# A selective-scan and mixture-of-experts block on one core: moving the z projection to the experts' idle PSUM banks, and the next sequence's norms and four GpSimd steps to other slots

## The chip, the core and the metric

The kernel runs on one core of a Trainium2 chip. The metric is the device time of one execution in microseconds (us). The core has TensorE (matmuls, results in the eight PSUM banks), VectorE, ScalarE and GpSimd for the element-wise work, and SyncE (SP), which issues the DMAs. Each engine runs its own list of instructions in order; between engines there are only semaphores.

## The reference

For each of 16 sequences of 512 rows and 128 columns:

```
h  = layernorm(x) * (1 + ca) + sa                    # sa, ca, ga, sb, cb, gb: one row each per sequence
xn = layernorm(h) * norm_g + norm_b
x  = x + ga * (h + mamba_f(xn) + flip(mamba_b(flip(xn))))
h  = layernorm(x) * (1 + cb) + sb
x  = x + gb * (sum over 8 experts, top 2 weighted, + one shared expert: (silu(h w1) * (h w2)) w3)

mamba(xn): u, z = split(xn Win);  u = silu(conv4(u));  dt_r, B, C = split(u Wx)
           dt = softplus(dt_r Wdt + b);  h_t = exp(dt_t A) h_(t-1) + dt_t u_t B_t   (256 channels x 16 states)
           y = (sum over states of h_t C_t + u D) * silu(z);  result y Wout
```

All data are 32-bit floats. silu(z) is computed as z/2 times (1 + tanh(z/2)); the factor one half is in the transposed weights wzT.

## The kernel before, in words

**Passes and slots.** The program runs 17 passes (`passes`, L303). Pass b does the scan of sequence b and, beside it, the experts of sequence b-1. A pass is a loop over 32 slots (STEPS), and each engine has its own copy of the loop (the functions `body`). A slot is one state n of one direction d: slots 0 to 15 are the forward direction, 16 to 31 the backward one. In the text "s29" is slot 29, and a slot runs from the start of its first scan on VectorE (L923) to the next slot's.

**What every slot has.** ScalarE writes exp(dt A) for the next slot into the two banks of psA (L675, one instruction for each half of the channels; each waits until VectorE has read that half). GpSimd multiplies v = dt u by a broadcast row of B into bt (L490), at most two slots ahead, because bt has two buffers. VectorE scans both halves in place (L923, twice), then multiplies each by a row of C into g (L933, twice). TensorE transposes g and adds it up in psY (L1181). SP loads the rows of B and C, two states with one DMA each (L389, L393).

**The experts.** In 18 of the slots TensorE computes an up projection into F0 and F1 (L1281, L1289; UP_SLOTS is 7 to 27 without 9, 10 and 22). One slot later ScalarE takes the tanh from F0 (L757) and copies F1 (L760), VectorE makes pf between its two read-outs (L1022), and GpSimd makes act (L580). The down projection goes to F2 (L1329). F0 and F1 hold nothing from s29 to s6.

**The preparation.** While a sequence is scanned, the next direction is prepared through one shared PSUM bank, psP, whose pieces are taken in a fixed order (pP_full, pP_free). PREP_SLOT is (19, 0): the forward direction of sequence b+1 is prepared from s19 of pass b, the backward one of sequence b from s0. Counted from there: u half 0 and half 1 at 0 to 5 (convolution as four matmuls, L1197; L693, L696; VectorE L963), the B, C and dt rows at 6 (L1205, L705), dt halves at 7 and 8 (L1210, L712 to L716), the logarithm at 9 (`ln1p`, L723, which loads a table of functions before it, and `preload_act_table` after it, L724), z halves at 9 and 11 (TensorE L1214 into psP, ScalarE tanh L696, VectorE zs one slot later, L963), dt at 10 on GpSimd (`make_dt`, L534), v at 11 (`make_v`, L539).

**The norms of sequence b+1** are also done in pass b: statistics on VectorE at s8 and s13 (L939, L943), their inverse roots on GpSimd at s9 and s14 (`moments`, L497 to L502), z1 and xn on ScalarE at s10 and s15 (L728), the modulation on GpSimd at s12 (L516, L518), the transposes and xnT at s16 (L1236, L745), hx on GpSimd at s21 (L522) and s23 (L525). The gated output weights wg are made on GpSimd at s25 (L595) from modG; SP's list has its DMA at s4, behind the loads of C rows that wait for the read-outs of s5 (L419, L393).

**Order inside a slot.** ScalarE: expert tanh and copy, exponentials of the next slot, ln1p, hxK, the experts' side work, then norms and preparation. GpSimd: bt of the next slot, then the output of sequence b-2 at s0, then `side` (wg, norms, dt, v), then `ffn_side` (act, xs). VectorE: two scans, first read-out, pf, second read-out, norms and preparation, the experts' side work, the gating of the forward direction. TensorE: sum of g of the slot before, the experts' side, down projection, post and preparation, up projection.

Of the kernel before, what the change touches and what calls it, by code (L numbers as in the profile page):

```python
# [21 lines left out]
U, XD, DT, Z = 0, 2, 3, 5  # L22
PREP = 7
# [55 lines left out]
def adaln_mamba_moe(nc, t, out):  # L79
# [3 lines left out]
    with ctx:  # L83
# [383 lines left out]
        def _(pool):  # L467
# [36 lines left out]
            def norms(b, slot):  # L504

                if slot == RSTD_SLOT:
                    if isinstance(b, int) and b == 0:
# [4 lines left out]
                if slot == H1_SLOT:
                    pool.wait_ge(zA, 8 * b + 4)
                    pool.wait_ge(modA_in, 16 * b + 16)
                    wait(pool, pP_full, xn_piece(b - 1) + 1)
                    g.tensor_tensor(xn[:, :, :], z1[:, :, :], over_tiles(modA[:, 1, :]), ALU.mult).then_inc(h1_s, 1)  # L516
                    pool.wait_ge(h1_s, 2 * b + 1)
                    g.tensor_tensor(z1[:, :, :], xn[:, :, :], over_tiles(modA[:, 0, :]), ALU.add).then_inc(h1_s, 1)  # L518
                if slot == HX_SLOT:

                    wait(pool, hxK_s, b)
                    g.tensor_tensor(hx[:, :, :], z1[:, :, :], over_tiles(modA[:, 2, :]), ALU.mult).then_inc(hx_s, 1)  # L522
                if slot == HX_SLOT + 2:
# [75 lines left out]
            def side(b, slot, prep_b, prep_f, post_f):  # L599
                if post_f and slot == WG_SLOT:  # L600
                    gated_weights(b)
                if prep_f is not None:
                    norms(prep_f, slot)
                    if slot == PREP_SLOT[0] + DT_AT + 3:
                        make_dt(prep_f, 0)
                    if slot == PREP_SLOT[0] + V_AT:
                        make_v(prep_f, 0)
                if prep_b and slot == PREP_SLOT[1] + DT_AT + 3:
                    make_dt(b, 1)
                if prep_b and slot == PREP_SLOT[1] + V_AT:  # L610
# [6 lines left out]
            norms(0, HX_SLOT)  # L617
            norms(0, HX_SLOT + 2)
# [25 lines left out]
        def _(act_e):  # L644
# [43 lines left out]
            def silu(b, d, kind, half):  # L688

                at = (0 if kind == U else 2) + half  # L690
                take(b, piece(d, kind, half))
                if kind == U:
                    s.activation(psP[:, :], psP[:, :], ACT.Identity, scale=0.5,  # L693
                                 bias=convb[d][:, half:half + 1]).then_inc(xh_s, 1)
                    act_e.wait_ge(xh_s, 4 * b + 2 * d + half + 1)
                s.activation(th[:, at, :], psP[:, :], ACT.Tanh).then_inc(th_s, 1)  # L696

            def prep(b, d, k):

                if k - U_AT in (1, 4):  # L700
                    silu(b, d, U, (k - U_AT) // 3)
# [15 lines left out]
                if k - Z_AT in (0, 2):  # L717
                    silu(b, d, Z, (k - Z_AT) // 2)
# [113 lines left out]
            first_z(F2[:, :], 0)  # L832
            first_z(psP[:, :], 1)
# [36 lines left out]
        def _(dve):  # L870
# [83 lines left out]
            def silu(b, d, kind, half):  # L954
                at = (0 if kind == U else 2) + half
                dve.wait_ge(th_s, 8 * b + 4 * d + at + 1)
# [5 lines left out]
                dst = (u if kind == U else zs)[d][:, half, :]  # L962
                w.scalar_tensor_tensor(dst, th[:, at, :], 1.0, psP[:, :], ALU.add, ALU.mult).then_inc(pP_free, 1)  # L963

            def prep(b, d, k):
                if k - U_AT in (2, 5):
                    silu(b, d, U, (k - U_AT - 2) // 3)
                if k - Z_AT in (1, 3):
                    silu(b, d, Z, (k - Z_AT) // 2)

            def gate_y(b, d, half):
# [8 lines left out]
                dve.wait_ge(pP_free, PIECES * b + piece(d, Z, 1) + 1)  # L980
# [164 lines left out]
        def _(pe):  # L1145
# [264 lines left out]
```

## Time and profile before

| what | value |
|---|---|
| device time, median of 3 runs | 2459.84 us (2459.71 to 2462.65) |
| the profiled execution's own time | 2461.73 us |
| its span, first to last instruction | 2459.9 us |
| VectorE busy | 2236.6 us, 91% |
| TensorE busy | 2066.5 us, 84% |
| GpSimd busy | 2023.6 us, 82% |
| ScalarE busy | 1511.4 us, 61% |
| DMA engines busy (mean) | some 37% |
| mean granted TensorE clock | 0.927 of 2.4 GHz |

How to read it: the shares are averages over stages with different limits. A line of the timeline gives the start, the duration, the engine and line of the kernel, the operation with result and operands, how many in a row are merged, and in brackets how long the engine had been idle before it and what ended the wait. Scans start 0.09 us before the instruction ahead of them has ended; so do most pairs on VectorE and ScalarE.

### The profile page before, as it was taken

The numbers are of one execution on the slowest core, as the hardware profiler recorded it, in microseconds if no ns is written. First come the engines' busy times: TensorE is split into PE (matmuls) and PEld (weight loads), VectorE is DVE, ScalarE is ACT, GpSimd is POOL, SyncE is SP. The second block draws the span as 40 slices with busy tenths as digits, with TensorE's granted clock in tenths as the row PEclk, the third lists the DMA queues.
The fourth block names the chain that finished last, engine by engine and source line by source line (L and its number), as shares of the span: only waits on it lengthen the run. The fifth ranks groups of instructions, "written<-read, shape, count | busy, mean of one in ns | idle before, by whom it ended". The sixth has DMA issues, their size and how long they took to land. (4 is left out here: it accounts for less than half of the span.)

```text
span 2459.9 us, 31865 instructions
## 1 busy us (share of the span) xinstructions
PE 2066.5 (84%) x9957; PEld 1312.1 (53%) x9957; DVE 2236.6 (91%) x3546; ACT 1511.4 (61%) x2483; POOL 2023.6 (82%) x1334
## 2 busy tenths in 40 slices
PE   6678988889888887978888898887978888898868
PEld 2445655545555554655555565554655555465545
DVE  4999999999999999999999999999999999999962
ACT  4656666576656666666676656666666576666633
POOL 2777979889798897979889797897979889797855
PEclk7678989989899999999999898999999999999989
DMA  5333343333444334333433334333433343333310
GB/s 149 131 136 122 134 135 132 136 122 126 135 133 135 122 126 134 135 134 129 140 123 125 134 130 143 126 121 126 140 134 127 133 129 125 129 135 136 123 67 27
DMA packets 124061, 312.42 MB, mean 127 GB/s; under 512 B 19700, under 2 KB 46308, under 8 KB 123892
## 3 DMA queue, kind: packets, MB, share of 16 engines
q1 hardware_dynamic: 123892, 310.39, 37.2%
q8 instruction: 79, 1.29, 0.2%
q14 instruction: 90, 0.74, 0.1%
HBM read 303.74 MB, written 6.60 MB: 126 GB/s over the span
## 5 line engine op out<-in xcount | busy, mean ns | idle before, releaser
L490 POOL TENSOR_TENSOR bt<-v,bb 128x1024 f32<-128x1024 f32 x511 | 1207.0, 2363 | 181.9 <-DVE psA L923 167.2
L923 DVE TENSOR_TENSOR_SCAN psA<-psA,bt 128x512 f32<-128x512 f32 x1024 | 1196.6, 1214 | 56.7 <-POOL bt L490 37.3
L675 ACT ACTIVATE psA<-dt,aneg 128x512 f32<-128x512 f32 x1024 | 689.3, 688 | 723.3 <-DVE g L933 723.1
L1181 PEld LDWEIGHTS psY<-ident,g 128*128 128x128 f32 x4096 | 509.4, 151 | 461.2 <-DVE g L933 256.0
L1181 PE MATMUL psY<-ident,g 128*128 128x128 f32 x4096 | 604.4, 292 | 166.4 <-DVE g L933 165.2
L933 DVE TENSOR_TENSOR g<-psA,cb 128x512 f32<-128x512 f32 x1024 | 672.6, 676 | 0.0
L580 POOL TENSOR_TENSOR act<-pf,gf 128x512 f32<-128x512 f32 x288 | 367.0, 1274 | 163.4 <-DVE pf L1022 151.0
L1281 PE MATMUL F<-h2T,w 128*128 128x512 f32 x576 | 325.5, 648 | 126.0 <-DVE pf L1022 125.9
L1329 PE MATMUL F<-w,act 128*128 128x128 f32 x2304 | 308.3, 277 | 13.6 <-POOL act L580 13.1
L1329 PEld LDWEIGHTS F<-w,act 128*128 128x128 f32 x2304 | 280.7, 192 | 31.1 <-POOL act L580 26.6
L1197 PE MATMUL psP<-xnT,wcT 128*128 128x512 f32 x496 | 258.2, 647 | 9.6 <-DVE zs L1085 9.2
L1022 DVE SCALAR_TENSOR_TENSOR pf<-tf,F 128x512 f32<-128x512 f32 x288 | 194.8, 676 | 42.5 <-ACT tf L757 40.2
L1281 PEld LDWEIGHTS F<-h2T,w 128*128 128x128 f32 x576 | 92.2, 192 | 229.9 <-DVE pf L1022 157.1
L757 ACT ACTIVATE tf<-F 128x512 f32<-128x512 f32 x288 | 170.5, 592 | 69.2 <-PE F L1281 68.9
L760 ACT ACTIVATE gf<-F 128x512 f32<-128x512 f32 x288 | 172.8, 600 | 52.8 <-PE F L1289 52.4
L1289 PE MATMUL F<-xs,w 128*128 128x512 f32 x320 | 164.3, 595 | 0.0
L1289 PE MATMUL F<-h2T,w 128*128 128x512 f32 x256 | 152.2, 681 | 0.0
L1197 PEld LDWEIGHTS psP<-xnT,wcT 128*128 128x128 f32 x496 | 93.5, 210 | 80.5 <-issue 79.5
L589 POOL TENSOR_TENSOR xs<-h2T,wB 128x512 f32<-128x512 f32 x80 | 101.9, 1274 | 8.7 <-DMA wB<-w_rows 8.7
L1289 PEld LDWEIGHTS F<-xs,w 128*128 128x128 f32 x320 | 61.1, 191 | 76.9 <-issue 76.9
L1289 PEld LDWEIGHTS F<-h2T,w 128*128 128x128 f32 x256 | 54.2, 212 | 70.6 <-issue 70.1
L1214 PE MATMUL psP<-xnT,wzT 128*128 128x512 f32 x124 | 70.7, 653 | 24.9 <-DVE zs L963 23.6
(185 smaller groups left out, 1936.4 us busy)
## 6 DMA issues: line engine op xcount, KB each, us to landing
bb<-bc_rows SPq DMA_DIRECT2D x256, 512.0 KB, 3.7
cb<-bc_rows SPq DMA_DIRECT2D x256, 512.0 KB, 3.6
wB<-w_rows SPq DMA_DIRECT2D x80, 256.0 KB, 3.9
x<-in_L_attn_x SPq DMA_DIRECT2D x16, 256.0 KB, 4.3
out_x<-osb SPq DMA_DIRECT2D x16, 256.0 KB, 4.5
modA<-mod_table SPq DMA_DIRECT2D x15, 192.0 KB, 4.4
w<-in_L_ffn_ew SPq DMA_DIRECT2D x2, 1024.0 KB, 7.6
bc_rows<-xd SPq DMA_DIRECT2D x32, 64.0 KB, 3.1
```

Source lines behind the costliest of these rows:

```text
L490: g.tensor_tensor(bt[:, n % 2, :, :], v[d][:, :, :], bb[:, n // 2 % 2, n % 2, :].unsqueeze(1).broadcast_to([P, NH, T]), ALU.mult).then_inc ...
L580: g.tensor_tensor(act[:, k // 2 % 3, k % 2, :], pf[:, k % 2, :], gf[:, k % 3, :], ALU.mult)\
L675: s.activation(psA[:, half * T:half * T + T], dt_[d][:, half, :], ACT.Exp, scale=aneg[d][:, half, n:n + 1]).then_inc(a_s, 1)
L760: s.activation(gf[:, k % 3, :], F1[:, :], ACT.Copy).then_inc(F1_free, 1)
L923: w.tensor_tensor_scan(ah, ah, bt[:, n % 2, half, :][:, order], 0.0, ALU.mult, ALU.add)\
L933: w.tensor_tensor(g_[:, n % 2, half, :], psA[:, half * T:half * T + T], cb[:, n // 2 % 2, n % 2, :], ALU.mult).then_inc(g_s, 1)
L1022: w.scalar_tensor_tensor(pf[:, k % 2, :], tf[:, k % 2, :], 1.0, F0[:, :], ALU.add, ALU.mult).then_inc(pf_s, 1)
L1181: last = m.matmul(psY[:, half * T + i * P:half * T + i * P + P], g_[:, n % 2, half, i * P:i * P + P], ident[:, :], is_transpose=True, star ...
L1197: last = m.matmul(psP[:, :], wcT[d][:, half, j, :], xnT[:, lo:lo + T], start=(j == 0), stop=(j == TAPS - 1))
L1281: m.matmul(F0[:, :], w1[:, x_, half * P:half * P + P], h2T[:, :], start=True, stop=True)\
L1289: m.matmul(F1[:, :], w2[:, x_, half * P:half * P + P], rows, start=True, stop=True)\
L1329: last = m.matmul(F2[:, i * D:i * D + D], act[:, e % 3, half, i * P:i * P + P], w3[:, ORDER[e], half, :], start=first, stop=final, skip_gr ...
```

## The change

The z pieces leave psP (PREP falls from 7 to 5 pieces for a direction). The forward z goes to F0 at s29 and F1 at s30, its zs is made at s30 and s31; the backward z goes to F0 at s2 and F1 at s5, both its zs are made at s6. Three semaphores (z_full, zt_s, z_free) take the place of pP_full, th_s and pP_free for z, and the first up projection of a pass waits for z_free. In the preamble z goes to F0 and F1 rather than F2 and psP. The norms of the next sequence move from s8 to s16 to s3 to s12. On GpSimd wg moves from s25 to s6, hx from s21 and s23 to s23 and s31, the backward v from s11 to s12. The wait of the transpose at s13 names the xn piece, and the wait for wtsT moves from XN_SLOT to s17, before the post pieces.

```diff
-U, XD, DT, Z = 0, 2, 3, 5
-PREP = 7
+U, XD, DT = 0, 2, 3
+PREP = 5
...
-U_AT, XD_AT, DT_AT, LN1P_AT, Z_AT, V_AT = 0, 6, 7, 9, 9, 11
-STAT_SLOT, RSTD_SLOT, Z1_SLOT, H1_SLOT, STAT2_SLOT, RSTD2_SLOT, XNORM_SLOT, XN_SLOT = 8, 9, 10, 12, 13, 14, 15, 16
-HX_SLOT, WG_SLOT = 21, 25
+U_AT, XD_AT, DT_AT, LN1P_AT = 0, 6, 7, 9
+V_SLOT = (30, 12)
+Z_SLOTS, ZS_SLOTS = ((29, 30), (2, 5)), ((30, 31), (6, 6))
+STAT_SLOT, RSTD_SLOT, Z1_SLOT, H1_SLOT, STAT2_SLOT, RSTD2_SLOT, XNORM_SLOT, XN_SLOT = 3, 4, 6, 7, 8, 9, 10, 12
+HX_SLOTS, WG_SLOT = (23, 31), 6
...
# GpSimd
-                if slot == HX_SLOT:
+                if slot == HX_SLOTS[0]:
...
-                if slot == HX_SLOT + 2:
+                if slot == HX_SLOTS[1]:
...
-                    if slot == PREP_SLOT[0] + V_AT:
+                    if slot == V_SLOT[0]:
                         make_v(prep_f, 0)
...
-                if prep_b and slot == PREP_SLOT[1] + V_AT:
+                if prep_b and slot == V_SLOT[1]:
                     make_v(b, 1)
...
# ScalarE
+            def turn_z(b, d, slot):
+
+                if slot in Z_SLOTS[d]:
+                    half = Z_SLOTS[d].index(slot)
+                    act_e.wait_ge(z_full, 4 * b + 2 * d + half + 1)
+                    s.activation(th[:, 2 + half, :], (F0, F1)[half][:, :], ACT.Tanh).then_inc(zt_s, 1)
...
-                if k - Z_AT in (0, 2):
-                    silu(b, d, Z, (k - Z_AT) // 2)
...
                     prep(prep_f, 0, slot - PREP_SLOT[0])
+                    turn_z(prep_f, 0, slot)
                 if prep_b:
                     prep(b, 1, slot - PREP_SLOT[1])
+                    turn_z(b, 1, slot)
...
# VectorE
+            def finish_z(b, d, slot):
+                for half in range(NH):
+                    if slot == ZS_SLOTS[d][half]:
+                        dve.wait_ge(zt_s, 4 * b + 2 * d + half + 1)
+                        w.scalar_tensor_tensor(zs[d][:, half, :], th[:, 2 + half, :], 1.0, (F0, F1)[half][:, :],
+                                               ALU.add, ALU.mult).then_inc(z_free, 1)
...
-                if k - Z_AT in (1, 3):
-                    silu(b, d, Z, (k - Z_AT) // 2)
...
-                dve.wait_ge(pP_free, PIECES * b + piece(d, Z, 1) + 1)
+                dve.wait_ge(z_free, 4 * b + 2 * d + 2)
...
                     prep(prep_f, 0, slot - PREP_SLOT[0])
+                    finish_z(prep_f, 0, slot)
                 if prep_b:
                     prep(b, 1, slot - PREP_SLOT[1])
+                    finish_z(b, 1, slot)
...
# TensorE
-                if k - Z_AT in (0, 2):
-                    half = (k - Z_AT) // 2
-                    open_piece(Z, half)
-                    m.matmul(psP[:, :], wzT[d][:, half, :], xnT[:, PAD:PAD + T], start=True, stop=True)\
-                        .then_inc(pP_full, 1)
+
+            def project_z(b, d, slot):
+
+                if slot in Z_SLOTS[d]:
+                    half = Z_SLOTS[d].index(slot)
+                    if d == 0:
+                        wait(pe, (pf_s, F1_free)[half], 2 * NE * (b - 1))
+                    else:
+                        pe.wait_ge(z_free, 4 * b + half + 1)
+                    m.matmul((F0, F1)[half][:, :], wzT[d][:, half, :], xnT[:, PAD:PAD + T], start=True, stop=True)\
+                        .then_inc(z_full, 1)
...
-                    pe.wait_ge(pP_free, min(PIECES * (fb + 1) + piece(1, Z, 1) + 1, PIECES * NB))
+                    if fb < NB - 2:
+                        pe.wait_ge(pP_free, xn_piece(fb + 2) + 1)
+                    else:
+                        pe.wait_ge(pP_free, min(PIECES * (fb + 1) + piece(1, DT, 1) + 1, PIECES * NB))
...
-                if slot == XN_SLOT:
+                if slot == POST_F_SLOT:
                     pe.wait_ge(wtsT_s, fb + 1)
...
                         pe.wait_ge(F2_free, free + H2T + 1)
+                        pe.wait_ge(z_free, min(4 * fb + 8, 4 * NB))
...
-            m.matmul(F2[:, :], wzT[0][:, 0, :], xnT[:, PAD:PAD + T], start=True, stop=True).then_inc(pP_full, 1)
-            m.matmul(psP[:, :], wzT[0][:, 1, :], xnT[:, PAD:PAD + T], start=True, stop=True).then_inc(pP_full, 1)
+            m.matmul(F0[:, :], wzT[0][:, 0, :], xnT[:, PAD:PAD + T], start=True, stop=True).then_inc(z_full, 1)
+            m.matmul(F1[:, :], wzT[0][:, 1, :], xnT[:, PAD:PAD + T], start=True, stop=True).then_inc(z_full, 1)
```

## Rows read from the trace of the kernel before

**Rows 1.** The waits: who waited for whom (us in total, times, longest).
```profile
DVE zs L963 <- ACT th L696: 49.3, 31, 1.6
...
DVE psA L923 <- POOL bt L490: 37.3, 60, 1.3
```
**Rows 2.** Timeline of VectorE, s29 and s30 of pass 8.
```profile
1340.76 2.33 DVE L923 TENSOR_TENSOR_SCAN psA<-psA,bt 128x512 f32<-128x512 f32 x2
...
1345.88 0.69 DVE L963 SCALAR_TENSOR_TENSOR zs<-th,psP 128x512 f32<-128x512 f32 x1 [1.61 <-ACT th L696]
1346.53 2.35 DVE L923 TENSOR_TENSOR_SCAN psA<-psA,bt 128x512 f32<-128x512 f32 x2
...
1350.57 1.22 DVE L923 TENSOR_TENSOR_SCAN psA<-psA,bt 128x512 f32<-128x512 f32 x1
```
**Rows 3.** Timeline of ScalarE, s29 of pass 8.
```profile
1341.58 1.28 ACT L723 ACT_TABLE_LOAD   x1
...
1345.25 0.60 ACT L696 ACTIVATE th<-psP 128x512 f32<-128x512 f32 x1
1345.74 1.30 ACT L675 ACTIVATE psA<-dt,aneg 128x512 f32<-128x512 f32 x2
```
**Rows 4.** Timeline of VectorE in pass 0: s8 (statistics), s9, start of s10.
```profile
80.47 2.35 DVE L923 TENSOR_TENSOR_SCAN psA<-psA,bt 128x512 f32<-128x512 f32 x2 [0.23 <-ACT psA L675]
...
85.11 2.31 DVE L923 TENSOR_TENSOR_SCAN psA<-psA,bt 128x512 f32<-128x512 f32 x2
...
88.83 1.23 DVE L923 TENSOR_TENSOR_SCAN psA<-psA,bt 128x512 f32<-128x512 f32 x1 [0.23 <-ACT psA L675]
```
**Rows 5.** The modG transfer: its issue in pass 9, and its landing time (DMA issues).
```profile
1379.98 0.43 SPq L419 DMA_DIRECT2D modG<-mod_table  x1
...
modG<-mod_table SPq DMA_DIRECT2D x16, 64.0 KB, 4.1
```
**Rows 6.** Timeline of VectorE, starts of s10 and s14 of pass 9.
```profile
1398.39 2.33 DVE L923 TENSOR_TENSOR_SCAN psA<-psA,bt 128x512 f32<-128x512 f32 x2
...
1418.18 1.23 DVE L923 TENSOR_TENSOR_SCAN psA<-psA,bt 128x512 f32<-128x512 f32 x1 [0.31 <-POOL bt L490]
```
**Rows 7.** Timeline of GpSimd, s12 and s13 of pass 9.
```profile
1411.96 1.28 POOL L516 TENSOR_TENSOR xn<-z,modA 128x512 f32<-128x512 f32 x1
...
1415.78 2.37 POOL L490 TENSOR_TENSOR bt<-v,bb 128x1024 f32<-128x1024 f32 x1
```
**Rows 8.** Timeline of TensorE, s12 and s13 of pass 9.
```profile
1411.50 1.13 PE L1281 MATMUL F<-h2T,w 128*128 128x512 f32 x2 [3.10 <-DVE pf L1022]
...
1413.91 1.91 PE L1181 MATMUL psY<-ident,g 128*128 128x128 f32 x8
```
**Rows 9.** Timeline of GpSimd, s21 of pass 8, then the group of act.
```profile
1308.92 1.30 POOL L522 TENSOR_TENSOR hx<-z,modA 128x512 f32<-128x512 f32 x1
...
L580 POOL TENSOR_TENSOR act<-pf,gf 128x512 f32<-128x512 f32 x288 | 367.0, 1274 | 163.4 <-DVE pf L1022 151.0
```
**Rows 10.** Timeline of VectorE, pass 8: starts of s23, s24, s27; pf of s28.
```profile
1313.81 2.35 DVE L923 TENSOR_TENSOR_SCAN psA<-psA,bt 128x512 f32<-128x512 f32 x2 [0.49 <-POOL bt L490]
...
1318.58 2.35 DVE L923 TENSOR_TENSOR_SCAN psA<-psA,bt 128x512 f32<-128x512 f32 x2 [1.25 <-POOL bt L490]
...
1331.82 2.35 DVE L923 TENSOR_TENSOR_SCAN psA<-psA,bt 128x512 f32<-128x512 f32 x2 [0.47 <-POOL bt L490]
...
1339.55 0.69 DVE L1022 SCALAR_TENSOR_TENSOR pf<-tf,F 128x512 f32<-128x512 f32 x1 [0.61 <-ACT tf L757]
```
**Rows 11.** Timeline of TensorE, s24 and s25 of pass 8.
```profile
1322.15 1.12 PE L1281 MATMUL F<-h2T,w 128*128 128x512 f32 x2 [1.69 <-DVE pf L1022]
...
1323.97 1.04 PE L1181 MATMUL psY<-ident,g 128*128 128x128 f32 x8
```
**Rows 12.** Engines by stretch, s24 to s28 of pass 8 (length; busy; granted clock; DMA).
```profile
1318.58:1340.76 22.18, 20.49 (x106) 12.95 (x105) 21.03 (x27) 15.90 (x28) 20.70 (x13) 1.00 0.37 126
```
**Rows 13.** Timeline of VectorE, s2 of pass 0.
```profile
60.77 0.69 DVE L963 SCALAR_TENSOR_TENSOR u<-th,psP 128x512 f32<-128x512 f32 x1 [0.96 <-ACT th L696]
```

More of the change, by code:

```diff
@@ L250, in adaln_mamba_moe @@
         th_s = sem("th_s")
+        z_full = sem("z_full")
+        z_free = sem("z_free")
+        zt_s = sem("zt_s")
         sp_s = sem("sp_s")
@@ L616, in _ @@
             pool.wait_ge(ga_in, 16)
-            norms(0, HX_SLOT)
-            norms(0, HX_SLOT + 2)
+            norms(0, HX_SLOTS[0])
+            norms(0, HX_SLOTS[1])
             pool.wait_ge(bt_s, 1)
@@ L686, in take, with silu @@
                 act_e.wait_ge(pP_full, PIECES * b + pos + 1)
[L688 to L696, printed above, removed]
+            def silu(b, d, half):
+                take(b, piece(d, U, half))
+                s.activation(psP[:, :], psP[:, :], ACT.Identity, scale=0.5,
+                             bias=convb[d][:, half:half + 1]).then_inc(xh_s, 1)
+                act_e.wait_ge(xh_s, 4 * b + 2 * d + half + 1)
+                s.activation(th[:, half, :], psP[:, :], ACT.Tanh).then_inc(th_s, 1)
+            def turn_z(b, d, slot):
[3 more added lines that the diff above has]
+                    s.activation(th[:, 2 + half, :], (F0, F1)[half][:, :], ACT.Tanh).then_inc(zt_s, 1)
             def prep(b, d, k):
                 if k - U_AT in (1, 4):
-                    silu(b, d, U, (k - U_AT) // 3)
+                    silu(b, d, (k - U_AT) // 3)
                 if k == XD_AT:
@@ L801, in first_z @@
             def first_z(bank, half):
-                act_e.wait_ge(pP_full, piece(0, Z, half) + 1)
-                s.activation(th[:, 2 + half, :], bank, ACT.Tanh).then_inc(th_s, 1)
+                act_e.wait_ge(z_full, half + 1)
+                s.activation(th[:, 2 + half, :], bank, ACT.Tanh).then_inc(zt_s, 1)
             norms(0, Z1_SLOT)
@@ L831, in _ @@
             exps(0, 0, 0, 0)
-            first_z(F2[:, :], 0)
-            first_z(psP[:, :], 1)
+            first_z(F0[:, :], 0)
+            first_z(F1[:, :], 1)
             act_e.wait_ge(const_ok, CONSTS)
@@ L952, in norms, with silu @@
                     statistics(z1, st, stat, lnA, 16 * b + 8)
-            def silu(b, d, kind, half):
-                at = (0 if kind == U else 2) + half
-                dve.wait_ge(th_s, 8 * b + 4 * d + at + 1)
+            def silu(b, d, half):
+                dve.wait_ge(th_s, 4 * b + 2 * d + half + 1)
                 if d == 0:
@@ L961, in silu @@
                     wait(dve, F2_full, (DOWN + NE) * (b - 1) + POSTB + half + 1)
-                dst = (u if kind == U else zs)[d][:, half, :]
-                w.scalar_tensor_tensor(dst, th[:, at, :], 1.0, psP[:, :], ALU.add, ALU.mult).then_inc(pP_free, 1)
+                w.scalar_tensor_tensor(u[d][:, half, :], th[:, half, :], 1.0, psP[:, :], ALU.add, ALU.mult)\
+                    .then_inc(pP_free, 1)
+            def finish_z(b, d, slot):
[4 more added lines that the diff above has]
+                                               ALU.add, ALU.mult).then_inc(z_free, 1)
             def prep(b, d, k):
                 if k - U_AT in (2, 5):
-                    silu(b, d, U, (k - U_AT - 2) // 3)
-                if k - Z_AT in (1, 3):
-                    silu(b, d, Z, (k - Z_AT) // 2)
+                    silu(b, d, (k - U_AT - 2) // 3)
             def gate_y(b, d, half):
@@ L1082, in first_z @@
             def first_z(bank, half):
-                dve.wait_ge(th_s, 2 + half + 1)
+                dve.wait_ge(zt_s, half + 1)
                 w.scalar_tensor_tensor(zs[0][:, half, :], th[:, 2 + half, :], 1.0, bank, ALU.add, ALU.mult)\
-                    .then_inc(pP_free, 1)
+                    .then_inc(z_free, 1)
             norms(0, STAT_SLOT)
@@ L1126, in body @@
                     if b == 0 and slot == 0:
-                        first_z(F2[:, :], 0)
-                        first_z(psP[:, :], 1)
+                        first_z(F0[:, :], 0)
+                        first_z(F1[:, :], 1)
                     if ffn:
@@ L1238, in side @@
                     prep(prep_f, 0, slot - PREP_SLOT[0])
+                    project_z(prep_f, 0, slot)
                 if prep_b:
                     prep(b, 1, slot - PREP_SLOT[1])
+                    project_z(b, 1, slot)
             def ffn_side(fb, slot):
```

## The prediction

> **What bounds the kernel now.** I read the waits first, then one steady pass slot by slot on each engine's timeline. Nearly all the time is in 16 scan passes; from pass 1 on they repeat, so I price one pass and multiply. VectorE's list is nearly full, and its work is the same before and after: instructions only move. So the change is worth what it does to VectorE's waits and to the 0.2 to 0.3 us lost at a slot's edge. The waits name two releasers [rows 1]: zs waits for ScalarE's tanh (49.3 us, 31 times, once in each half pass), and the scans wait for GpSimd's bt (37.3 us). The timelines show what stands behind them. In s29 zs waits 1.61 us [rows 2] for a tanh that stands on ScalarE behind ln1p: two table loads and a logarithm, from 1341.58 until the tanh can start at 1345.25 [rows 3]. GpSimd's list is late at s14 (0.31 us) [rows 6] and at s23, s24 and s27 (0.49, 1.25, 0.47 us) [rows 10].
>
> **The edge of a slot.** A slot with nothing behind the second read-out lasts 3.72 to 3.75 us, with a 0.23 us wait in it, since the next exponential is not ready sooner [rows 4]. With one 0.68 us instruction behind it, it lasts 1350.57 - 1346.53 = 4.04 us [rows 2]: the first costs 0.3 us, a second its full 0.60 us (0.69 less an overlap of 0.09). With a set of statistics a slot without experts lasts 85.11 - 80.47 = 4.64 us [rows 4], 0.9 more than bare and 1.2 more than the 3.44 us at which the read-outs end. A slot with pf alone lasts 4.03 us (one instruction more than bare, too); there the edge is hidden, and what is taken away gives all of its 0.6 or 1.2 us.
>
> **Part 1, z at s29 to s31.** The naive reading is that the 1.61 us wait goes. It doesn't: the exponentials of s30 stand behind the same ln1p. They can start where the tanh did, at 1345.25 [rows 3]. From an exponential's start to the scan that it feeds it was 1346.53 - 1345.74 = 0.79 us [rows 2, 3], so the scan starts at 1346.04 and s29 lasts 5.28 us instead of 5.77: 0.49 gained, and VectorE idles some 1.7 us there for another reason. The zs of half 0 now follows in s30, beside the experts' sum: 0.60 lost. That of half 1 stays in s31. Sum: +0.11 us.
>
> **Part 2, z at s2, s5 and s6.** The two matmuls and tanh lie in slots in which TensorE and ScalarE have room; both zs follow the read-outs of s6, which was bare: 0.3 + 0.6 = +0.9 us. Between s6 and the exponential due 2.96 us into s7 ScalarE has the second exponential, hxK, h2T, the four z1 (0.48 us each) and xd; I add them up to 2.8 us into s7. Cost 0; as the margin is small, bound 0 to 0.5 us.
>
> **Part 3, statistics.** s3 was bare: +0.9 us [rows 4]. Those of s13 become those of s8, those of s8 those of s3, so s8 is as before. x's DMA is issued behind the read-outs of s1 and three small issues of 0.43 us, some 1.3 us into s2; with modG's landing time, 4.1 us [rows 5], it is there 0.8 us into s3 (an estimate), and the statistics start 3.4 us into it.
>
> **Part 4, GpSimd at s6 to s9.** wg waits for modG, whose DMA is issued 0.12 us before s6 starts (1380.10) and lands 4.1 us later [rows 5]. So wg runs from 4.0 to 5.3 us of s6, and the bt behind it ends 3.0 us into s7, due 2.3 us later. Then the modulation, 2.6 us, and the next bt, done 2.6 us into s8; act is wanted there at 3.6, and from then on the list is as before. SP's row loads wait up to 3 us longer for these bt and land a slot ahead of need. hx at s31 (1.3 us) is followed by the output's two steps; the bt of s2 is ready with 0.5 us in hand, and the stores and the load of x are held by the read-outs of s1 anyway. Cost 0, bound 0 to 0.5 us.
>
> **Part 5, s10 to s13.** Before: 1418.18 - 1398.39 = 19.79 us [rows 6]. VectorE after: s10 5.28 (ln1p as in part 1), s11 3.75, s12 4.03 (zs gone), s13 4.03 (statistics gone), 17.09 us. GpSimd works without a break from before s10 to the bt of s14, and the two modulation steps (1.28 each, 0.03 between) leave that stretch: 2.59 us. That bt then ends at 1418.15 - 2.59 = 1415.56 [rows 7], and s14 can start at 1415.59: 17.20 us. The later one decides: 2.59 us gained. v at s12 instead of s11 changes places with a bt that isn't due yet. TensorE: it idles 3.10 us in s12, and the eight transposes of s13 then take 1.91 us [rows 8] instead of 1.04 [rows 11]: its lower level, 1.2 GHz. With s12 and s13 shorter by 2.2 us it comes to s14's slots about 0.3 us late, which pf there can bear. I take 0 for it, bound 0 to 1.0 us.
> The Trainium skill (TensorE: Matmul & The Clock Gate, Part 1) says that an idle array's clock is halved and comes back only after sustained work. By that page the lower level could last through the up projection of s13, which now has 1.6 us less before its pf is due; the part would then give 1.7 instead of 2.6 us. The trace has that projection at full speed; the sum goes by it.
>
> **Part 6, s21 to s23.** GpSimd's hx (1.30 us) leaves s21 [rows 9], so s23 starts 0.49 us earlier, and 0.08 more that the wait hid: 0.57. The bt of s24 now comes at the end of a chain that starts with the pf of s22: pf ends 3.51 us into the slot, then act and xs of 1.27 us each [rows 9] and bt of 2.37 [rows 7], 8.4 us with small gaps. Before, s22 and s23 took 1318.58 - 1313.81 + 4.03 + 0.57 = 9.37 us [rows 10]. So s24 starts 0.94 us earlier, a good half of its waits.
>
> **Part 7, s24 to s28.** wg (as long as hx) leaves s25, and the 0.47 us wait at s27 goes [rows 10]. I count it at nothing. Behind the pf of s24 (idle 1.69 us before 1322.15) [rows 11] TensorE works without a break: 20.49 of 22.18 us, at a granted clock of 1.00 [rows 12]. Its dt matmuls release ScalarE's Abs, Relu, Exp and, behind them, the tanh for which the pf of s28 waits 0.61 us [rows 10]. Nothing in that chain is moved. s27 begins 0.55 us earlier, and the pf waits grow by 0.55 us.
>
> **The sum for one pass:** 0.11 + 0.9 + 0.9 - 2.59 - 0.94 = -1.62 us, -1.67 with the terms unrounded. Passes 1 to 14: 23.4 us. Pass 0 has no experts: s3 and s6 +1.8, s10 and s29 -1.0, s12 -0.3, s13 -0.9, s30 +0.3; and as psP isn't held by z at its start, u's 0.96 us wait in s2 [rows 13] goes with its overlap, -1.1: together -1.2 us. Pass 15 has no norms: s6 +0.9, s10 -0.8, s12 -0.6, and a late bt behind wg -0.8: -1.3 us. Pass 16 has only experts. In all 26 us. The profiled execution took 2461.73 us (1.8 more than its span): 2435.7. The median of the runs is 1.9 us below it: 2433.8 us.
>
> **Rivals.**
> *Part of the gain* (0.12): TensorE or ScalarE becomes the bound in s6 to s8 or s12 to s14. The bounds of parts 2, 4 and 5 add to 2.0 us; half of that, 0.5 to 1.0 us a pass, makes it 2441 to 2448 us. The page's rule in part 5 (0.9 us a pass, 2446 us) is in it with 0.04. For it: margins of 0.1 to 0.5 us. Against: each is positive by the rows.
> *More* (0.10): the wait at s27 is a real gain of 0.55 us a pass, if the matmul ends, which the profile models, show TensorE later than it is: 2426 us. Against: pf's 0.61 us wait in s28.
> *Slower* (0.04): the clock in s24 to s28. Eight transposes take 1.04 us there and 1.91 us at the lower level [rows 8, 11], so 1 us of full-speed work becomes 1.84, and this stretch has no slack. From 2.0 us of its work at 1.2 GHz the 1.67 us are gone; with 4.0 us a pass is 1.7 us slower than before, 2484 us. Against: full clock in this stretch now, and the change doesn't add to TensorE's idle time ahead of it.
> *No change* (0.04): the new z semaphores hold something that no row shows, or these effects cancel, about 2460 us.
> The forecast has 0.70.
>
> A measurement of this kernel can tell about 0.2% (5 us) from no change. Faster by more than that: the forecast, the partial and the larger gain, 0.92; within: 0.04; slower: 0.04. The range reaches down to the larger gain less 2 us of rounding over 14 passes, 2424, and up to a partial gain of 0.8 us a pass less, 2446.
>
> **What would show it.** zs's wait for tanh gone from the list, and scans that wait for ScalarE instead, some 1.7 us at s29 and s10; s29 at 5.28, s30 4.63, s3 4.64, s6 4.63; s10 to s13 at 17.2; the wait at s23 gone, that at s24 0.6 us; s24 to s28 still at 22.2 us, with pf waiting more in s27; a pass at 145.2 us instead of 146.9. It is wrong if a pass takes over 146 or under 144.5 us, or if a bt is late in s7 to s9.

## The result and the profile after

The changed kernel takes 2439.7 us (median of 4 runs, 2437.7 to 2440.2), the kernel before on the same chip 2459.8 us: ratio 0.991 [0.990, 0.993]. The prediction was 2433.8 us, with a range from 2424 to 2446. The gain is 20.1 us where 26 were forecast.

The profiled execution took 2439.4 us with a span of 2437.6 us. From its page and its list of waits (who waited for whom: us in total, times, longest):

```profile
span 2437.6 us, 31806 instructions
...
PE 2059.1 (84%) x9957; PEld 1314.2 (54%) x9957; DVE 2230.6 (92%) x3546; ACT 1513.4 (62%) x2483; POOL 2023.6 (83%) x1334
...
DVE psA L933 <- ACT psA L680: 67.7, 88, 1.8
...
DVE pf L1036 <- ACT tf L767: 50.0, 51, 5.1
...
DVE psA L933 <- POOL bt L495: 14.7, 18, 0.9
```

The same list before had, beside the rows of [rows 1]:

```profile
DVE pf L1022 <- ACT tf L757: 40.2, 33, 5.1
...
DVE psA L923 <- ACT psA L675: 18.8, 80, 0.3
```

The 49.3 us in which zs waited for tanh are gone from the list, and the scans wait for ScalarE's exponentials instead, 67.7 us where it was 18.8: nearly the whole wait has only changed its name. The wait for bt fell from 37.3 to 14.7 us [rows 1]. VectorE has the same 3546 instructions as before.

s29 and s30 of pass 8, VectorE and then ScalarE:

```profile
1324.83 2.34 DVE L933 TENSOR_TENSOR_SCAN psA<-psA,bt 128x512 f32<-128x512 f32 x2
...
1330.11 2.35 DVE L933 TENSOR_TENSOR_SCAN psA<-psA,bt 128x512 f32<-128x512 f32 x2 [1.77 <-ACT psA L680]
...
1333.55 0.68 DVE L978 SCALAR_TENSOR_TENSOR zs<-th,F 128x512 f32<-128x512 f32 x1
...
1334.75 2.34 DVE L933 TENSOR_TENSOR_SCAN psA<-psA,bt 128x512 f32<-128x512 f32 x2
```
```profile
1325.66 1.28 ACT L731 ACT_TABLE_LOAD   x1
1326.95 1.06 ACT L731 ACTIVATE ab<-ab 128x1024 f32<-128x1024 f32 x1
1328.03 1.28 ACT L732 ACT_TABLE_LOAD   x1
1329.32 1.30 ACT L680 ACTIVATE psA<-dt,aneg 128x512 f32<-128x512 f32 x2
```

It is the picture of [rows 2, 3] with the exponential in the tanh's place: s29 lasts 1330.11 - 1324.83 = 5.28 us, s30 4.64.

Slot lengths, mean over passes 1 to 14, in us; the slots that are not in the table moved by at most 0.04:

| slot | before | forecast | after |
|---|---|---|---|
| s3 (statistics) | 3.74 | 4.64 | 4.63 |
| s6 (zs twice) | 3.75 | 4.63 | 4.62 |
| s10, s11, s12 | 5.81, 3.72, 4.63 | 5.28, 3.75, 4.03 | 5.28, 3.75, 4.04 |
| s13 | 5.62 | 4.14 | 4.32 (4.10 to 4.63) |
| s22, s23 | 4.59, 4.77 | 0.94 less in sum | 4.03, 4.41 |
| s26, s27 | 4.58, 4.21 | s27 +0.55 | 4.03, 4.76 |
| s24 to s28 in sum | 22.18 | 22.18 | 22.18 |
| s29, s30 | 5.77, 4.04 | 5.28, 4.63 | 5.29, 4.63 |
| whole pass | 146.96 | 145.29 | 145.56 (145.2 to 146.1) |

Of the 22.3 us between the two profiled executions passes 1 to 14 give 19.5, pass 0 2.1, pass 15 0.4; the preamble to the first scan is 2.6 shorter (47.9 to 45.3) and the tail behind the last scan's start 2.2 longer (86.9 to 89.1). Variants of the changed kernel with this same preamble and tail (runs 5, 6 and 9 to 12) had 45.3 to 48.0 us and 87.0 to 89.0 us, so I don't count these two as the change's.

**What s13 shows.** Engines by stretch (length; busy of PE, PEld, DVE, ACT, POOL; granted clock; DMA share; GB/s), s13 of passes 2, 3, 4 and 8:

```profile
378.06:382.69 4.63, 4.63 (x12) 2.45 (x12) 4.11 (x6) 3.26 (x6) 4.63 (x4) 0.50 0.29 105
524.27:528.70 4.43, 4.43 (x17) 2.32 (x17) 4.11 (x6) 3.26 (x6) 4.43 (x4) 0.69 0.23 66
669.81:673.91 4.10, 4.10 (x14) 2.48 (x13) 4.10 (x6) 3.17 (x5) 4.10 (x4) 0.58 0.25 90
...
1252.15:1256.27 4.12, 3.39 (x18) 1.95 (x17) 4.11 (x6) 3.05 (x5) 4.12 (x4) 1.00 0.27 81
```

TensorE around it, pass 2 and then pass 8. An up projection is two matmuls in the program, one into F0 and one into F1, and the profile shows each as two:

```profile
377.60 2.07 PE L1309 MATMUL F<-h2T,w 128*128 128x512 f32 x2 [2.66 <-DVE pf L1036]
379.47 1.91 PE L1317 MATMUL F<-h2T,w 128*128 128x512 f32 x2
381.17 1.91 PE L1197 MATMUL psY<-ident,g 128*128 128x128 f32 x8
...
1251.69 1.13 PE L1309 MATMUL F<-h2T,w 128*128 128x512 f32 x2 [2.66 <-DVE pf L1036]
1252.65 1.02 PE L1317 MATMUL F<-h2T,w 128*128 128x512 f32 x2
```

Behind the same 2.66 us of idling the same up projection takes 3.78 us in pass 2, from 377.60 to 381.38, and 1.98 in pass 8: 1.2 GHz and 2.4 GHz. ScalarE and VectorE in pass 2:

```profile
381.41 0.60 ACT L770 ACTIVATE gf<-F 128x512 f32<-128x512 f32 x1 [1.11 <-PE F L1317]
381.91 1.29 ACT L680 ACTIVATE psA<-dt,aneg 128x512 f32<-128x512 f32 x2
...
382.69 2.35 DVE L933 TENSOR_TENSOR_SCAN psA<-psA,bt 128x512 f32<-128x512 f32 x2 [0.53 <-POOL bt L495]
```

ScalarE idles 1.11 us before gf, the exponentials of s14 stand behind it (the first ends at about 382.6), and the scan waits. In that pass GpSimd is late as well, and not from s13 but from s8. GpSimd in pass 2, then in pass 8:

```profile
359.87 1.27 POOL L585 TENSOR_TENSOR act<-pf,gf 128x512 f32<-128x512 f32 x1 [1.93 <-DVE pf L1036]
361.09 2.36 POOL L495 TENSOR_TENSOR bt<-v,bb 128x1024 f32<-128x1024 f32 x1
...
380.25 2.35 POOL L495 TENSOR_TENSOR bt<-v,bb 128x1024 f32<-128x1024 f32 x1
...
1233.44 1.27 POOL L585 TENSOR_TENSOR act<-pf,gf 128x512 f32<-128x512 f32 x1 [0.89 <-DVE pf L1036]
```

s8 begins at 355.70 and 1229.84, so this act starts 4.17 us into s8 in pass 2 and 3.60 in pass 8. pf was there in both; in pass 2 gf ended only 4.04 us into s8, since the up projection of s8 ran at the lower level (granted clock 0.61 in s8, 0.86 in pass 8). From this act to the bt of s14 GpSimd has no gap, so the 0.5 us arrives there. There are two ways, then, and the runs below take one away. In seven passes s13 lasts over 4.4 us; in six of these the scan of s14 waits for the exponentials, and only in pass 2 for bt.

### The profile page after: what moved, and what is told of

Its sections match the earlier page's. It is cut to its first block and busy times, and to the rows that moved or that the text cites. A ratio compares the mean times of both kernels' runs of the same rounds, so it can differ in the third digit from the quotient of the medians.

```text
span 2437.6 us, 31806 instructions
## 1 busy us (share of the span) xinstructions
PE 2059.1 (84%) x9957; PEld 1314.2 (54%) x9957; DVE 2230.6 (92%) x3546; ACT 1513.4 (62%) x2483; POOL 2023.6 (83%) x1334
## 5 line engine op out<-in xcount | busy, mean ns | idle before, releaser
L933 DVE TENSOR_TENSOR_SCAN psA<-psA,bt 128x512 f32<-128x512 f32 x1024 | 1196.0, 1213 | 83.1 <-ACT psA L680 67.7
L1309 PE MATMUL F<-h2T,w 128*128 128x512 f32 x576 | 329.5, 656 | 96.2 <-DVE pf L1036 95.7
L1317 PE MATMUL F<-h2T,w 128*128 128x512 f32 x256 | 154.1, 688 | 0.0
L1226 PE MATMUL psP<-xd,wdtT 8*128 8x512 f32 x124 | 77.0, 703 | 17.8 <-ACT xd L715 16.5
```

Of the source, the lines that this page charges most:

```text
L933: w.tensor_tensor_scan(ah, ah, bt[:, n % 2, half, :][:, order], 0.0, ALU.mult, ALU.add)\
L1309: m.matmul(F0[:, :], w1[:, x_, half * P:half * P + P], h2T[:, :], start=True, stop=True)\
L1317: m.matmul(F1[:, :], w2[:, x_, half * P:half * P + P], rows, start=True, stop=True)\
```

## The experiments

"Pass" is the mean of passes 1 to 14 in the one profiled execution of each run. The kernel before took 2462.7 to 2463.6 us on the chips of these runs, and the changed kernel was timed only beside the 2459.8 us of the result, so differences of a few us between these runs and the 2439.7 us are read from the slots and not from the times.

**1. The z part alone.** F0 and F1 for z, as in the change; norms and GpSimd steps as before.

```diff
# from the change
+Z_SLOTS, ZS_SLOTS = ((29, 30), (2, 5)), ((30, 31), (6, 6))
...
# against the changed kernel
-V_SLOT = (30, 12)
+V_SLOT = (30, 11)
...
-HX_SLOTS, WG_SLOT = (23, 31), 6
+HX_SLOTS, WG_SLOT = (21, 23), 25
```

> Only the z pieces move to F0 and F1; norms and GpSimd steps stay where they were before. My theory (s10 to s13 are set by GpSimd's list, which keeps the modulation at s12): s6 +0.9 us a pass, s29 -0.5, s30 +0.6, and the 1.1 us that VectorE saves at s10 and s12 turns into a longer wait for bt at s14, so s10 to s13 stay at 19.8 us. A pass takes about 147.9 us, 1.0 us more than before: 2459.8 + 13 = about 2473 us. The naive rival (the tanh waits were the cost, 1.6 us each, and go with z): 2459.8 - 50 = about 2410 us. A middle rival (VectorE's own sum counts everywhere): -0.1 us a pass, 2458 us.

Measured: 2479.2 us, ratio 1.007 [1.005, 1.009], pass +1.33 us. s6, s10, s29 and s30 are as forecast; s10 to s13 last 19.76 us in sum, no less than before (19.78). The scans of s13 and s14 in pass 3:

```profile
529.82 2.34 DVE L933 TENSOR_TENSOR_SCAN psA<-psA,bt 128x512 f32<-128x512 f32 x2 [0.48 <-POOL bt L495]
...
535.94 2.35 DVE L933 TENSOR_TENSOR_SCAN psA<-psA,bt 128x512 f32<-128x512 f32 x2 [0.80 <-POOL bt L495]
```

What z leaves free on VectorE is waited away for GpSimd, as the sum of Part 5 has it. Alone this part makes the kernel slower; the 0.3 us beyond the forecast 1.0 is mostly at s15 (5.06 to 5.42 on average). It is there in five passes alone, with 6.06 or 6.07 us each; in pass 2 the up projection of s15 takes 3.68 us, the lower level, and the experts' sum (facc) waits 0.91 us for TensorE.

**2. The norms alone.** Norms at s3 to s12, z in psP.

```diff
-STAT_SLOT, ..., XN_SLOT = 8, 9, 10, 12, 13, 14, 15, 16
+STAT_SLOT, ..., XN_SLOT = 3, 4, 6, 7, 8, 9, 10, 12
```

> Only the norms move (s3 to s12); z stays in psP, GpSimd's wg, hx and v stay. Theory: s3 +0.9 us; the modulation leaves GpSimd's stretch before s14, so s10 to s13 fall from 19.8 to VectorE's own 18.2 us (z still there), and as the xn transposes now wait in TensorE's list for the last zs out of psP at the end of s12, up to 0.5 us of that comes back in s13. A pass -0.2 to -0.7 us: 2450 to 2457 us. Rival (the transposes behind zs hold the up projections and cost more than 1.5 us at s13): 2465 us or more, slower than before.

Measured: 2486.4 us, ratio 1.009 [1.006, 1.011], pass +1.75 us. My theory missed this; the rival had it. TensorE and VectorE in pass 3 (s13 begins at 537.83):

```profile
538.05 1.09 PE L1236 MATMUL psP<-ident,xn 128*128 128x128 f32 x4 [4.38 <-DVE zs L963]
538.93 1.92 PE L1284 MATMUL F<-h2T,w 128*128 128x512 f32 x2
540.64 1.91 PE L1292 MATMUL F<-h2T,w 128*128 128x512 f32 x2
...
541.52 0.69 DVE L1022 SCALAR_TENSOR_TENSOR pf<-tf,F 128x512 f32<-128x512 f32 x1 [0.77 <-ACT tf L757]
...
543.87 1.23 DVE L923 TENSOR_TENSOR_SCAN psA<-psA,bt 128x512 f32<-128x512 f32 x1 [1.07 <-ACT psA L675]
```

psP is held by z until the zs at the end of s12. The transposes of xn stand behind it, and the up projection of s13 behind them: TensorE idles 4.38 us, then works at 1.2 GHz, and both pf and the exponentials of s14 are late. So z had to leave psP before the norms could move.

This is s13, which lasts 5.93 us where VectorE's own sum is 4.03. Another 0.6 us of the loss are in s8 (5.50) and s9 (4.31), and they go with the clock: only in passes 2, 3, 7, 11 and 12, where it is 0.50 or 0.51 in s8, does s8 last 5.9 to 6.1 us and s9 4.8 to 5.0 (elsewhere 5.2 and 4.0), and in pass 3 pf waits 0.62 and 0.84 us for its tanh there. The four runs took from 2479.7 to 2493.1 us and the profiled one is the slowest, with a tail of 93.5 us instead of 86.9, so that the 1.75 us may be high.

**3. The GpSimd steps alone** (wg to s6, hx to s23 and s31, backward v to s12).

```diff
-HX_SLOT, WG_SLOT = 21, 25
+HX_SLOT, WG_SLOT = 23, 6
```

> Only the GpSimd steps move (hx to s23 and s31, wg to s6, backward v to s12). Theory: s22 and s23 together -0.94 us a pass as hx leaves s21; s26 -0.55 but s27 +0.55; s10 to s13 unchanged at 19.8: 14 x -0.94 = -13 and some -1 for the last pass: 2446 us. Rival (the wait at s27 counts too): 2438 us. Rival (wg's wait for modG at s6 holds bt and gives it back): about 2460 us.

Measured: 2450.1 us, ratio 0.995 [0.993, 0.997], pass -0.93 us, as forecast; s22 4.03, s23 4.42, s26 4.03, s27 4.76.

**4. z and norms, GpSimd steps as before.**

```diff
-V_SLOT = (30, 12)
+V_SLOT = (30, 11)
...
-HX_SLOTS, WG_SLOT = (23, 31), 6
+HX_SLOTS, WG_SLOT = (21, 23), 25
```

> The changed kernel with its GpSimd steps back where they were (hx at s21 and s23, wg at s25, backward v at s11): z and the norms move together. The parts alone gave, per pass, z +1.33 us, norms +1.75, GpSimd steps -0.93, which would add up to 2.2 us slower, while all together gave -1.39. Theory: z and the norms need each other (z must leave psP before the xn transposes can stand at s12, and the modulation must leave GpSimd's list before VectorE's savings at s10 to s13 count), and the GpSimd steps are independent of both: a pass at about 145.56 + 0.93 = 146.5 us, s10 to s13 at 17.4, s22 and s23 at 9.36 again: about 2453 us. Rival (the GpSimd moves are what makes the norms work, by freeing GpSimd): a pass above 147.5 us, 2467 us or more.

Measured: 2458.0 us, ratio 0.998 [0.997, 0.999], pass -0.21 us, s10 to s13 17.69. Parts that cost 1.33 and 1.75 us alone give 0.21 together: 3.3 us a pass is their interplay (3.1 by the medians). The GpSimd steps on top give 1.18, not the 0.93 that they give alone, so this run lies between its theory (2453 us) and the rival. The difference is in s12, which stays at 4.61 us. The scan of s13 in pass 9:

```profile
1407.24 2.35 DVE L933 TENSOR_TENSOR_SCAN psA<-psA,bt 128x512 f32<-128x512 f32 x2 [0.50 <-POOL bt L495]
```

v stands at s11 here, and the bt of s13 behind it is late by 0.47 to 0.50 us in every pass. With v at s12 (runs 5 and 6) s12 lasts 4.04. Part 5 says that v "changes places with a bt that isn't due yet" and leaves it at that; the 17.20 us need this move, and without it s10 to s13 are 0.3 us longer than with the whole change.

**5. hx back**, in the changed kernel.

```diff
-HX_SLOTS, WG_SLOT = (23, 31), 6
+HX_SLOTS, WG_SLOT = (21, 23), 6
```

> The changed kernel with hx's two steps back at slots 21 and 23 instead of 23 and 31. Part 6's theory: slot 22 back to 4.59 us and slot 23 to 4.77 us, together 0.9 us a pass slower; pass 146.5 us, time 2453 us. Rival (hx at slot 31 also costs something at slots 1 to 3 of the next pass, or the gain of 22 and 23 is given back at slots 24 to 28 in part): a pass 146.0 us or less, time at most 2446 us.

Measured: 2454.2 us, ratio 0.996 [0.995, 0.998]. s22 and s23 cost 0.91 us of the pass's 1.03: Part 6, to 0.03 us.

**6. wg back**, in the changed kernel.

```diff
-HX_SLOTS, WG_SLOT = (23, 31), 6
+HX_SLOTS, WG_SLOT = (23, 31), 25
```

> The changed kernel with the gated weights back at slot 25 and nothing else. Part 7 of the prediction says that their leaving slot 25 is worth nothing, since TensorE and ScalarE bound slots 24 to 28: then these five slots last 22.18 us in sum as with the change (slot 26 4.6 instead of 4.03, slot 27 4.2 instead of 4.76), the pass stays at 145.5 to 145.6 us and the time at 2438 to 2441 us. GpSimd has 1.3 us less to do at slots 6 to 8, where it wasn't late: nothing there. Rival (the matmul ends are modelled, and GpSimd did bound slot 27): slots 24 to 28 last 22.7 us, a pass 146.1 us and the time 2447 us.

Measured: 2439.1 us, ratio 0.991 [0.989, 0.992], pass 145.50 (-0.06). s24 to s28 of pass 8, changed kernel and then this one:

```profile
1302.65:1324.83 22.18, 20.98 (x107) 13.13 (x106) 20.93 (x27) 16.23 (x28) 19.51 (x12) 1.00 0.37 128
```
```profile
1304.01:1326.19 22.18, 20.98 (x107) 13.13 (x106) 21.04 (x27) 16.25 (x28) 20.73 (x13) 1.00 0.37 126
```

GpSimd has 1.2 us more to do, and the five slots last the same. Part 7's nothing is shown, and the larger gain (the second rival of the prediction) has fallen.

**7. No logarithm.** A copy takes the place of the logarithm, and both table loads go (softplus isn't computed).

```diff
-                s.activation(ab[:, :, :], ab[:, :, :], ACT.Ln, bias=1.0).then_inc(sp_s, 1)
-                s.preload_act_table(ACT.Exp)
+                s.activation(ab[:, :, :], ab[:, :, :], ACT.Copy).then_inc(sp_s, 1)
```

> The changed kernel with the logarithm of the softplus replaced by a plain copy on ScalarE and without the two table loads, so 2.6 us less of ScalarE in s10 and s29 (softplus is not computed, the work otherwise the same). Theory: at s29 VectorE waits for the exponentials behind ln1p, so s29 falls from 5.29 to about 3.75 us; s10 falls likewise but GpSimd's list to s14 doesn't get shorter, so s10 to s13 together stay within 0.2 us of 17.2 to 17.4 with the wait moved to a bt. A pass -1.5 to -1.7 us: 2439.7 - 22 = about 2417 us. Rival (both slots count): 2396 us. Rival (ln1p is hidden, the wait at s29 has another cause): 2439 us.

Measured: 2423.6 us, ratio 0.984 [0.982, 0.985], pass -0.67 us. s29 and s10 fall to 3.75 us each, so ScalarE was their bound. But s10 to s13 last 17.21 us (after: 17.39), and the end of this stretch is GpSimd's:

```profile
1394.04 2.37 POOL L495 TENSOR_TENSOR bt<-v,bb 128x1024 f32<-128x1024 f32 x1
...
1396.44 1.23 DVE L932 TENSOR_TENSOR_SCAN psA<-psA,bt 128x512 f32<-128x512 f32 x1 [1.03 <-POOL bt L495]
```

That is the 17.20 us of Part 5. Less came out than expected (a pass -1.5 to -1.7 us, about 2417 us) because s1, s9 and s31 then grew (+0.6, +0.25, +0.2). In s1 it is GpSimd again: in pass 8 the scan of s2 waits 0.56 us for a bt that stands behind hx's second step and the two steps of the output, whose margin Part 4 put at 0.5 us.

**8. Extra matmuls at s10 to s12**, into psP, read by nothing: the first of the two ways (idle, then low clock in s13) is taken away.

```diff
+                if prep_f is not None and slot in (10, 11, 12):
+                    wait(pe, pP_free, xn_piece(prep_f))
+                    for _ in range(slot - 9):
+                        m.matmul(psP[:, :], wcT[0][:, 0, 0, :], xnT[:, PAD:PAD + T], start=True, stop=True)
```

> The changed kernel with extra matmuls into the free bank psP in TensorE's idle time (one in s10, two in s11, three in s12, of 128x512; their results are overwritten by the xn transposes). Theory: the passes differ (145.2 to 146.1 us) by the slots s13 and s14, where TensorE is at its lower clock behind its idle time in s12 and pf or the exponentials wait for it. With the idle time filled, s13 stays at 4.1 us in every pass; mean pass 145.3 instead of 145.56, 14 x 0.3 = 4 us less: 2435.5 us. Rival (the clock has nothing to do with it, the spread is chance in DMA or semaphores): 2439.7 us, s13 scattered as before. Rival (the extra matmuls are in the way of the up projections): slower, 2445 us or more.

Measured: 2436.9 us, ratio 0.990 [0.989, 0.992], pass -0.17 us. s13 of passes 2, 3 and 8:

```profile
378.67:383.30 4.63, 3.90 (x19) 2.22 (x18) 4.11 (x6) 3.54 (x6) 4.63 (x4) 1.00 0.29 105
524.58:528.72 4.14, 3.41 (x18) 1.98 (x17) 4.11 (x6) 3.06 (x5) 4.14 (x4) 1.00 0.20 80
1251.53:1255.67 4.14, 3.41 (x18) 1.97 (x17) 4.11 (x6) 3.06 (x5) 4.14 (x4) 1.00 0.17 67
```

The clock is 1.00 in s13 of all 14 passes, and s13 is 4.13 to 4.19 us in 11 of them. In the other three (passes 2, 5, 10: 4.63, 4.33, 4.26) act started 4.17, 4.05 and 3.98 us into s8 instead of 3.6: the second way. Both ways are shown, the first is the larger: with it gone s13 is 4.20 on average instead of 4.32. The times alone wouldn't show it, as the four runs (2436.3 to 2441.0 us) overlap with those of the changed kernel.

**9. z1's statistics at s10**, what hangs on them at s14 to s16.

```diff
-STAT_SLOT, ..., STAT2_SLOT, RSTD2_SLOT, XNORM_SLOT, XN_SLOT = 3, ..., 8, 9, 10, 12
+STAT_SLOT, ..., STAT2_SLOT, RSTD2_SLOT, XNORM_SLOT, XN_SLOT = 3, ..., 10, 14, 15, 16
```

> The changed kernel with the second half of the norms later: statistics of h at s10 instead of s8, their roots at s14, xn at s15, transposes at s16 (those three where they were before the change). Theory: VectorE idles 1.7 us in s10 behind ln1p, so the statistics cost nothing there, and s8 gets 1.2 us shorter; TensorE's and ScalarE's work between s7 and s9 gives 0.3 us of it back in s9, as in the last pass, which has no norms. s10 stays 5.3. A pass -0.9 us: 2439.7 - 12 = about 2428 us. Rival (GpSimd's list to s14 is the bound from s8 on, and gives all back at s13): 2440 us.

Measured: 2438.7 us, ratio 0.991 [0.989, 0.992], pass -0.15 us: a miss. s8 gives 0.92, but s9 takes back 0.52 (in pass 3 the pf of s9 waits 0.96 us for its tanh) and s13 0.24. The rival had the time (2440 us) but only part of the place, since it put all of the loss at s13.

**10. x's statistics at s29 of the pass before**, with x in two buffers and loaded a pass ahead.

```diff
-        x = sb("x", [P, NT, D])
+        x = sb("x", [P, 2, NT, D])
...
+                if slot == EARLY_STAT and b + 1 < NB:
+                    first_norm(b + 1)
```

> The changed kernel with two buffers for x: x is loaded one pass ahead, and its statistics are made in s29 of the pass before instead of in s3. Theory: VectorE idles 1.7 us in s29 behind ln1p, the 1.2 us of statistics fit, s29 stays at 5.3 us, s3 falls from 4.63 to 3.75: -0.88 us a pass, 2439.7 - 12 = about 2428 us. Rival (s29 isn't idle for the reason that I give, and the statistics lengthen it): 2440 us.

Measured: 2430.6 us, ratio 0.987 [0.986, 0.989], pass -0.75 us. s3 falls to 3.77 us and s29 stays at 5.28: the statistics are free in the 1.77 us in which VectorE waits for the exponentials. s13 is 4.44.

**11. The same with extra matmuls** at s5 (three, into F2) and s10 to s12.

> The kernel with x in two buffers and its statistics at slot 29 of the pass before (144.82 us a pass, 2430.6 us), plus the extra matmuls that nothing reads (3 into F2 at slot 5, 1, 2 and 3 into psP at slots 10 to 12). If TensorE's low clock is what makes slot 13 last 4.44 us there: slot 13 4.1 to 4.2 us, a pass 144.4 to 144.6 us, time 2425 to 2427 us. Rival (GpSimd's bt or ScalarE decides in slot 13, as pass 2 of the kernel with extra matmuls at 10 to 12 showed, and the extra matmuls stand before what is needed): no gain, 144.8 us and 2430 us or more.

Measured: 2426.1 us, ratio 0.985 [0.983, 0.986]. The time is in the theory's range, the pass is not: 144.74 us, only 0.08 less than run 10. s13 has clock 1.00 throughout and still a mean of 4.32, because act starts up to 4.17 us into s8: the rival was right on s13. That the time is in the range is luck: of the 3.4 us between the profiled executions of runs 10 and 11 passes 1 to 14 give only 1.1, pass 0 1.0 and the tail 1.2.

**12. Runs 9 and 10 together, with the extra matmuls of run 11.**

> The changed kernel with x in two buffers and loaded a pass ahead, x's statistics at slot 29 of the pass before, z1's statistics at slot 10 (what hangs on them at 14 to 17), and extra matmuls that nothing reads: 3 into F2 at slot 5, 1, 2 and 3 into psP at slots 10, 11, 12. Theory: slot 3 3.75 us (-0.87), slot 8 4.3 us (-0.9), slot 9 at 4.1 to 4.6 us if its delay was TensorE's low clock (+0.1 to +0.5), slots 10 to 13 17.4 to 17.7 us: a pass 143.9 to 144.3 us, time 2416 to 2422 us. Rival (slot 9 is held by GpSimd's and ScalarE's order, not by the clock, and gives back what slot 8 gives, as in the run with statistics at slot 10 alone): a pass 144.7 us, time 2428 us.

Measured: 2417.8 us, ratio 0.982 [0.980, 0.983], pass 143.92 us, as the theory had it. s3 3.77, s8 4.25, s13 4.11 to 4.14 in every pass; s9 4.44 on average, and 5.27 and 5.28 in passes 7 and 12. s7 and s8 in sum, pass 7 and then pass 2:

```profile
1066.76:1076.20 9.44, 7.58 (x22) 4.18 (x22) 9.31 (x29) 7.73 (x15) 8.13 (x6) 0.69 0.27 92
348.99:358.33 9.34, 7.48 (x24) 3.97 (x24) 9.24 (x30) 7.64 (x15) 8.21 (x6) 0.82 0.27 90
```

In pass 7, with a granted clock of 0.69, the pf of s9 then waits 1.14 us for its tanh. This version beats both kernels, the changed one by some 22 us (24 by their ratios to the kernel before).

## Why the prediction was right

By its steps:

- **Parts 1, 2, 3**: each slot within 0.02 us. The naive gain of 1.6 us in s29 didn't come, since the exponentials stand behind the same logarithm; run 7 shows it by taking that away.
- **Part 4** (0, bound 0 to 0.5): s7 and s8 as before, s9 0.04 us longer, and no bt late in s7 to s9. s9 is 4.19 us in passes 3, 11 and 14, those with the lowest granted clock in s8 (0.54): in pass 3 the eight transposes of s8 take 1.91 us, the dt matmuls behind them come late, and with them ScalarE's chain to the tanh of s9.
- **Part 5** (-2.59): -2.39 measured. The GpSimd bound of 17.20 us is met in the passes with s13 at 4.11 us and in run 7. The step that was mis-sized is its last term: "I take 0 for it, bound 0 to 1.0 us", on the ground that "the trace has that projection at full speed". It measured 0.19 us in s13 and 0.04 in s14; with the 0.04 of s9 that is 0.27 us a pass and 3.9 us of the 6 that are missing from the gain. (Another 2.2 is how the profiled executions lie to their medians: 1.9 us above before, 0.3 below after.) The ground was a single row of a single pass, and it was misread. Of that up projection [rows 8] show the matmul into F0 alone; the one into F1 took 1.65 us, where full speed is 1.02:

```profile
1412.46 1.65 PE L1289 MATMUL F<-h2T,w 128*128 128x512 f32 x2
```

  The trace of before has the lower level in s13 of passes 1 to 3 too, and part of s13 in seven others, here pass 2 and pass 6:

```profile
384.26:389.86 5.60, 5.60 (x18) 3.30 (x17) 5.26 (x15) 3.27 (x6) 5.52 (x5) 0.60 0.32 121
...
971.85:977.45 5.60, 4.27 (x21) 2.38 (x20) 5.26 (x15) 3.47 (x7) 5.52 (x5) 1.00 0.31 121
```

  Both last 5.60 us: with the statistics in s13 the low clock was covered, and the change took the cover away. In the changed kernel the clock is below 1.00 in s13 of 12 passes of 14 and costs 0.3 to 0.5 us in 7 of them (in pass 2 together with the late act). The rule of the Trainium skill weighed there (TensorE: Matmul & The Clock Gate, Part 1) agrees with the trace in kind: fully in passes 2, 5 and 13 (3.78 us), not at all in 8 and 10 (1.98 us). The 0.9 us a pass that the prediction worked out was over three times the 0.27 measured. Only three passes have the lower level all through the up projection, and even there s13 is only 0.5 us longer, because a late up projection costs only what it lacks behind GpSimd's bt.
- **Part 6** (-0.94): -0.92. The scan of s24 still waits 0.90 us for bt; the 0.6 us given for it doesn't follow from the part's own sum, which leaves 1.25 - (0.94 - 0.57) = 0.88. **Part 7** (0): 0, s27 longer by the 0.55 us that s26 and the wait lost.
- **Pass 0**: -2.1 instead of -1.2. s2, s3, s6, s10, s29 and s30 came as priced; s17 gave 0.9 that I hadn't priced (5.51 to 4.60). **Pass 15**: -0.4 instead of -1.3; s13 and s14, priced at nothing, grew by 0.8 there. These two cancel by luck, as do the 2.6 us of the preamble and the 2.2 of the tail.

Of the rivals, "part of the gain" named the right place; the outcome, 0.3 us a pass, lies between the forecast's 0 and its 0.5. "Slower" had the clock fall in s24 to s28, where it is 1.00 in all 14 passes. That each part alone can be slower than before (runs 1 and 2) was in no rival: I priced the parts one by one, and the sum held only because Part 5 was read as one stretch with both z and the statistics gone from it.

## What to carry to other kernels

Before a term is set to zero on a row of one pass, look at that stretch in every pass: the granted clock of a stretch differs from pass to pass though the instructions don't, and work that the change takes away can be what covered it. Moves that share a queue (here psP) are not to be priced apart: one part can be what allows the other, and each alone a loss. And a wait that stays (here 1.8 us of VectorE at s29) is the place to put other work: the statistics cost 0.9 us in a bare slot and nothing there.

## What the runs showed of the hardware

- Behind one and the same idle of TensorE, 2.66 us, the same up projection (four matmuls of 128x512 in the profile) took 1.98 us in two passes and 3.78 us in three, and between these in the other nine. In the kernel before, behind 3.10 us, it took 1.98 us in four passes and 3.78 in three, so the longer idle was not the more often followed by the lower level. What decides it no row shows.
- With matmuls in the idle time (run 8) the clock was 1.00 in s13 of all 14 passes. The extra work cost s13 0.02 to 0.03 us and gave back more.
- A table load takes 1.28 us, and the instruction behind it starts 0.01 us after its end (64 of the 65 loads in the trace of the changed kernel; 0.38 us after the other): the load, the logarithm and the load back are 3.66 us with no further pause.
